# Router of a mixture-of-experts layer: split weights side by side in one stationary tile, ranks in five products

## The reference

```python
logits = xf @ Wr                                   # 4096 x 256 times 256 x 8
probs = jax.nn.softmax(logits, axis=-1)
topk_p, topk_i = jax.lax.top_k(probs, TOP_K)       # 2 of 8
topk_p = topk_p / jnp.sum(topk_p, axis=-1, keepdims=True)
gate = gate.at[jnp.arange(N)[:, None], topk_i].add(topk_p)
for e in range(N_EXPERTS):
    h = new_gelu(xf @ Wfc[e] + bfc[e]) @ Wproj[e] + bproj[e]
    routed = routed + h * gate[:, e:e + 1]
```

## Time and profile before

| what | value |
|---|---|
| median of 3 runs | 934.13 us (933.46 to 935.68) |
| the profiled execution | 939.65 us, its span 938.0 us |
| PE busy in the span | 901.5 us (96%) |
| DVE, ACT, POOL busy | 611.6, 518.8, 338.4 us |
| share of the last chain | PE 86%, DVE 7%, issue 3% |

### The profile page before, as it was taken

The page is one execution under the profiler, slowest core; times in us unless marked ns, Lnnn a source line. Parts: engine busy times, 40 slices in busy tenths (PEclk is TensorE's granted clock), DMA queues, the critical chain, the costliest instruction groups (busy, mean ns, idle before and its releaser), DMA issues.

```text
span 938.0 us, 20267 instructions
## 1 busy us (share of the span) xinstructions
PE 901.5 (96%) x6934; PEld 794.0 (85%) x6943; DVE 611.6 (65%) x1457; ACT 518.8 (55%) x1050; POOL 338.4 (36%) x318
## 2 busy tenths in 40 slices
PE   6999998999998999999999899999999999999996
PEld 4688995566655788888889899999999999999996
DVE  4898796898877766666555655565565656565442
ACT  3693433665546355546444666575666657575552
POOL 3467222211311554544453224233242423332222
PEclk9999999999999999999999899999999999999998
DMA  8300020000002111111237245225252522522222
GB/s 240 123 1 1 1 91 1 2 1 1 2 16 84 49 71 59 65 60 59 77 114 249 58 135 135 47 45 136 46 136 46 136 46 46 136 46 46 46 46 35
DMA packets 48943, 64.00 MB, mean 68 GB/s; under 512 B 9984, under 2 KB 41920, under 8 KB 48768
## 3 DMA queue, kind: packets, MB, share of 16 engines
q0 software_dynamic: 17504, 34.87, 16.0%
q1 hardware_dynamic: 31248, 27.46, 9.9%
q10 hardware_dynamic: 144, 1.05, 0.4%
HBM read 38.59 MB, written 24.77 MB: 68 GB/s over the span
## 4 chain that ended last, share of the span: by engine, by line
PE 86%; DVE 7%; issue 3%; ACT 1%; DMA 1%; POOL 1%; SPq 1%; DVEq 0%; POOLq 0%; ACTq 0%
PE PS L136 24%; PE PS L137 23%; PE PS L138 23%; PE PS L877 3%; PE PS L1833 2%; PE PS L306 2%; PE PS L907 1%; PE PS L921 1%; PE PS L927 1%; DVE mxpad L1121 1%; DVE hidl L142 1%; PE PS L287 1%; DMA xr<-routed_rows 1%; PE PS L1360 1%; PE PS L849 1%
## 5 line engine op out<-in xcount | busy, mean ns | idle before, releaser
L1879 ACT ACTIVATE hideh<-PS,be 128x256 fp32r<-128x256 f32 x280 | 140.5, 502 | 154.2 <-PE PS L138 139.5
L1907 POOL DMA_INDIRECT out_rows<-y,toki x70 | 122.9, 1755 | 270.4 <-DVE y L1947 261.3
L142 DVE TENSOR_TENSOR hidel<-act32e,hideh 128x256 fp32r<-128x256 f32 x280 | 118.4, 425 | 107.5 <-ACT act32e L1881 95.3
L136 PE MATMUL PS<-xTeh,wfch 128*128 128x256 f32 x560 | 159.4, 285 | 1.7 <-issue 1.1
L136 PE MATMUL PS<-wprh,hideh 128*128 128x256 f32 x560 | 159.0, 284 | 0.0
L137 PE MATMUL PS<-xTel,wfch 128*128 128x256 f32 x560 | 158.4, 283 | 0.0
L138 PE MATMUL PS<-xTeh,wfcl 128*128 128x256 f32 x560 | 158.4, 283 | 0.0
L138 PE MATMUL PS<-wprh,hidel 128*128 128x256 f32 x560 | 155.9, 278 | 0.0
L137 PE MATMUL PS<-wprl,hideh 128*128 128x256 f32 x560 | 155.9, 278 | 0.0
L1881 ACT ACTIVATE act32e<-PS,be 128x256 f32<-128x256 f32 x280 | 140.9, 503 | 2.8 <-DVE hidel L142 2.8
L136 PEld LDWEIGHTS PS<-xTeh,wfch 128*128 128x128 f32 x560 | 107.3, 192 | 3.3 <-issue 2.6
(11 more groups left out here) (273 smaller groups left out, 2086.3 us busy)
## 6 DMA issues: line engine op xcount, KB each, us to landing
xr<-routed_rows SPq DMA_DIRECT2D x36, 272.0 KB
fcraw<-in_Wfc POOLq DMA_DIRECT2D x8, 1024.0 KB
prraw<-in_Wproj POOLq DMA_DIRECT2D x8, 1024.0 KB
X<-in_x SPq DMA_DIRECT2D x8, 512.0 KB, 6.6
out_rows<-X SPq DMA_DIRECT2D x8, 512.0 KB, 2.9
routed_rows<-pads SPq DMA_DIRECT2D x8, 272.0 KB
out_rows<-y,toki POOLq DMA_INDIRECT x70
ctx<-in_ctxT SPq DMA_DIRECT2D x4, 256.0 KB, 6.5
```

The lines of the kernel that those rows point to most:

```text
L136: nc.tensor.matmul(out, wh, xh, start=first, stop=False)
L142: return eng.tensor_tensor(out, whole, high.bitcast(F32), ALU.subtract)
L1879: nc.scalar.activation(hid[0][:, j, :], PS[:, j % 4, 0:BLK], ACT.Gelu_apprx_tanh, bias=bias)
L1907: nc.gpsimd.indirect_dma_start(out=out, out_offset=bass.IndirectOffsetOnAxis(ap=toki[:, h:h + 1], axis=0), in_=y[:, h, :], in_offset=None, ...
```

## The change

Two edits. (1) The high and low router weights lie side by side in `both_wr`, 16 columns, and each half of the input is multiplied with all 16: four TensorE products for a batch instead of six (low x low, left out before, is now computed too). `lT` has 16 rows, its transposes 16 columns, and `choose` adds the two halves with a reduction out of PSUM where it copied before. (2) `both` gets a fifth tile that stays zero (a memset in `next_setup`). `ranks` is one product of `both` with the triangle over 40 columns, and then, for each tile s, one product with ones whose moving operand is tile s repeated over all later tiles and the totals (32, 24, 16 and 8 columns). They go to bank 4 instead of 5.

```diff
-            wrp = [early("wr" + n, [P, KD, E], F32R) for n in "hl"]
+            both_wr = early("both_wr", [P, KD, 2 * E], F32R)
...
-            both = early("both", [P, TB, E], BF16)
+            both = early("both", [P, TB + 1, E], BF16)
...
-            lT = late("lT", [E, L])
+            lT = late("lT", [2 * E, L])
...
                 def logits(b):
                     pe.wait_ge(hT_ready, KD * b + KD)
-                    for k in range(KD):
-                        last = product(PS[0:E, 4, :], [w[:, k, :] for w in wrp],
-                                       [x[:, k, :] for x in xTs[b % 2]], k == 0, k == KD - 1)
+                    for i, x in enumerate(xTs[b % 2]):
+                        for k in range(KD):
+                            last = nc.tensor.matmul(PS[0:2 * E, 4, :], both_wr[:, k, :], x[:, k, :],
+                                                    start=i + k == 0, stop=i + k == KD)
...
-                        last = nc.tensor.transpose(PS[:, 5, t * E:(t + 1) * E], lT[0:E, t * P:(t + 1) * P],
-                                                   ident[0:E, 0:E])
+                        last = nc.tensor.transpose(PS[:, 5, 2 * t * E:2 * (t + 1) * E], lT[0:2 * E, t * P:(t + 1) * P],
+                                                   ident[0:2 * E, 0:2 * E])
...
                 def ranks(b):
                     pe.wait_ge(chosen, b + 1)
-                    for t in range(TB):
-                        for s in range(t + 1):
-                            last = nc.tensor.matmul(PS[:, 5, (TB + t) * E:(TB + t + 1) * E],
-                                                    triones[:, 0 if s == t else 1, :], both[:, s, :],
-                                                    start=s == 0, stop=s == t)
+                    end = (TB + 1) * E
+                    nc.tensor.matmul(PS[:, 4, 0:end], triones[:, 0, :], both[:], start=True, stop=False,
+                                     skip_group_check=True)
                     for s in range(TB):
-                        last = nc.tensor.matmul(PS[:, 5, 2 * TB * E:(2 * TB + 1) * E], triones[:, 1, :], both[:, s, :],
-                                                start=s == 0, stop=s == TB - 1)
+                        last = nc.tensor.matmul(PS[:, 4, (s + 1) * E:end], triones[:, 1, :],
+                                                both[:, s:s + 1, :].to_broadcast([P, TB - s, E]),
+                                                start=False, stop=s == TB - 1, skip_group_check=True)
...
                 def choose(b):
-                    nc.vector.tensor_copy(lg[:, 0, :, :].rearrange("p t e -> p (t e)"),
-                                          PS[:, 5, 0:TB * E]).then_inc(l_read, 1)
+                    nc.vector.tensor_reduce(lg[:, 0, :, :],
+                                            PS[:, 5, 0:2 * TB * E].rearrange("p (t c e) -> p t e c", c=2, e=E),
+                                            op=ALU.add, axis=AX).then_inc(l_read, 1)
...
                 def next_setup():
+                    nc.vector.memset(both[:], 0.0)
```

More of the change, by code:

```diff
@@ L1492, in evac_logits @@
                     act.wait_ge(lT_psum, b + 1)
-                    nc.scalar.activation(lT[0:E, :], PS[0:E, 4, :], ACT.Copy).then_inc(lT_ready, 1)
+                    nc.scalar.activation(lT[0:2 * E, :], PS[0:2 * E, 4, :], ACT.Copy).then_inc(lT_ready, 1)
                 def whole(b, first=2):
@@ L1622, in choose @@
                     link(nc.vector.tensor_tensor(m4[:, 2, :], m4[:, 0, :], m4[:, 1, :], ALU.subtract))
-                    nc.vector.tensor_tensor(both[:], oh[:, 0, :, :], oh[:, 1, :, :],
+                    nc.vector.tensor_tensor(both[:, 0:TB, :], oh[:, 0, :, :], oh[:, 1, :, :],
                                             ALU.add).then_inc(chosen, 1)
@@ L1643, in place_rows @@
                     link(nc.vector.tensor_tensor(pos,
-                                                 PS[:, 5, TB * E:2 * TB * E].rearrange("p (t e) -> p t e", e=E),
+                                                 PS[:, 4, 0:TB * E].rearrange("p (t e) -> p t e", e=E),
                                                  carry[:].unsqueeze(1).to_broadcast([P, TB, E]), ALU.add))
-                    nc.vector.tensor_tensor(carry[:], carry[:], PS[:, 5, 2 * TB * E:(2 * TB + 1) * E],
+                    nc.vector.tensor_tensor(carry[:], carry[:], PS[:, 4, TB * E:(TB + 1) * E],
                                             ALU.add).then_inc(r_read, 1)
@@ L1692, in next_split @@
                     dve.wait_ge(wr_in, 16)
-                    nc.vector.tensor_copy(wrp[0][:], wr[:]).then_inc(wr_split, 1)
+                    nc.vector.tensor_copy(both_wr[:, :, 0:E], wr[:]).then_inc(wr_split, 1)
                     dve.wait_ge(wr_split, 1)
-                    low(nc.vector, wrp[1][:], wr[:], wrp[0][:]).then_inc(wr_split, 1)
+                    low(nc.vector, both_wr[:, :, E:2 * E], wr[:], both_wr[:, :, 0:E]).then_inc(wr_split, 1)
                 o_low, att_residual, invert_sums, turn_back, divide = attention[4](dve, next_setup, next_rows, next_split)
```

## The result

The changed kernel takes 932.06 us, median of 20 runs (928.59 to 935.81). The kernel before, in 20 runs beside it, takes 935.50 us (932.79 to 937.38). The ratio is 0.9969, 95% interval 0.9957 to 0.9981: 2.9 us faster (1.8 to 4.0); the two medians lie 3.4 us apart. The forecast was 4.9 us less, 929.2 us, range 926.8 to 931.5, so the time lies 2.9 us above the forecast and 0.6 us above the range.

The account below looks back on a forecast made before the run. TensorE was taken to bound six batches, alternating with VectorE in the first part. Terms 3.7 (logits) + 1.5 (ranks) - 0.1 - 0.1 - 0.1 gave 4.9 us less than 934.13: 929.2 us, range 926.8 to 931.5.

Parts of the forecast that it names:

- 0.463 + 0.21 - 0.02: Savings per batch on TensorE: two fewer logits products 0.463 us, cheaper ranks 0.21, less 0.02 for wider transposes.
- rival C: The five rank products don't pipeline, 166 ns each instead of 30: 934.0 us, no change; chance 0.03.
- rival E: Loads of the rank products are not hidden, nine fewer save 0.86 us a batch: 924.7 us; chance 0.01.
- the unknown terms: Bounds of the uncertain small costs, other than serial ranks: together 0.5 us down and 0.8 up.
- At nothing: Parts counted as costing 0: the 16-row copy, the halves of `both_wr`, bank 4 for the ranks; scattering called untouched.
- this margin: Slack between the gate behind ScalarE's `copy_rows` and VectorE's need of it after `place_slots`; expected to hold, no size given.
- the logits and ranks of batch 1 as on the chain: Batch 1's TensorE savings counted in full: logits in eight batches, 3.7 us; ranks in seven, 1.5 us.
- transposes of batch 2 about 1 us earlier: A sign on TensorE's timeline that the forecast holds, beside the routed stage starting 4.9 us earlier.
- Scattering is not touched: The 16 row copies and DMAs of a batch keep their place behind the slots; counted as no cost.
- rival A: The stall behind the ranks of batch 1 goes, 1.5 us more saved: 927.7 us; chance 0.19.
- rival B: A pause and low clock of that kind elsewhere, costing 1.7 to 3.2 us: 930.9 to 932.4 us; chance 0.10.
- Rival D: Thinner router work lowers TensorE's clock in every batch, 1.7 us a fall: 939.4 us with six; chance 0.03.

Follow-up runs that it names:

- e7_before: The kernel before again, no edit, one run with a second trace: 935.92 us.
- e8_after: The changed kernel again, no edit, one run: 928.94 us.
- e9_after: The changed kernel again, no edit, on another chip: 931.91 us against 938.81 for the kernel before beside it, ratio 0.9927.
- e12_before_filler: The kernel before with 18 unread TensorE products of 256 columns ahead of the transposes of batch 2, as control: ratio 0.9996 to the kernel before.
- e3_again: The changed kernel again, no edit: 932.42 us against 934.95 for the kernel before beside it, ratio 0.9977.
- filler runs: 18 unread TensorE products ahead of the transposes of batch 2: in the changed kernel 930.86 and 932.73 us, in the kernel before ratio 0.9996.
- e4_double: The changed kernel with two buffers for `rows` and `slotc`: 929.48 us, ratio 0.9951 to the kernel before.
- e10_double: The changed kernel with two buffers for `rows` and `slotc`, repeated on another chip: 929.04 us, ratio 0.9908 to the kernel before.
- e14_shift_double: The changed kernel with two buffers plus 24 unread products of 8 columns ahead of the ranks of batch 0: 930.21 us.
- e13_shift: The changed kernel with 24 unread products of 8 columns ahead of the ranks of batch 0: 931.62 us against 932.90 for the changed kernel.
- e15_after: The changed kernel again, no edit: 932.90 us against 935.89 for the kernel before beside it, ratio 0.9976.

## Why the prediction was wrong

**The terms of the sum were right.** A batch was to shrink by 0.463 + 0.21 - 0.02 = 0.65 us and shrank by 0.68; the halves alone read 0.44 and 0.24. The rank products cost 28 ns each on average (0.14 us for five), so they take nothing extra for the repeated operand: rival C's 166 ns is excluded. The Trainium skill's formula for LDWEIGHTS ("TensorE: Matmul & The Clock Gate") gives 107 ns for the load of 128 columns that each has; the trace does not agree that each product takes that long, and rival E, which would have taken 0.86 us off a batch in the ranks' half where 0.24 went, is excluded with it. Two slips in the prediction's sums change nothing in the forecast: with 107 ns and its own seven batches the sum would be near 10 us and not near 11; and the unknown terms add up to about 1.0 us up and not 0.8 (0.3 for the logits, 0.1 for the ranks, 0.3 for the transposes, 0.3 for the first step of the choice).

**The step that failed** is the last sentence of the paragraph "At nothing": "VectorE needs the gate only behind all of `place_slots`, and I expect this margin to hold", and with it the counting of the logits and ranks of batch 1 as on the chain. The prediction named the margin and put no number on it. There was none: the list of waits of the kernel before shows no wait for `hn` in the profiled execution and 0.2 us in e7_before, which means TensorE and the scatter's chain arrived nearly together. From there what TensorE saves in batch 1 turns into a wait: the batch was to shrink by 0.65 us and grew by 0.56 (e7_before to e8_after). The forecast "transposes of batch 2 about 1 us earlier" came out 0.8 later (336.01 against 335.20); each of the two traces has one stretch at 1.2 GHz ahead of that point, from 289 and from 329 us, so the clock does not explain it. Between e7_before and e8_after it was 0.4 us earlier, after the transposes of batch 1 had been 1.0 earlier (311.94 against 312.92).

**"Scattering is not touched"** was the second half of this error. GpSimd's instructions are the same, but the load of TensorE's instructions is a transfer too, and the change moved it onto the scatter. In the traces of the changed kernel the scatter comes 0.7 to 1.3 us later for it, at the only place where TensorE hangs on a scatter: in its first trace the scatter of batch 1 takes even 4.63 us, and TensorE has no wait for it.

**The stretch behind the ranks of batch 1** (rival A) did not settle as one case. A pause of TensorE there was in the traces of e7_before, e9_after, e12_before_filler and others, and in none of the four kernels taken on the chip of e3_again, changed or half changed. Where it is absent, the wait for `hn` is longer (2.7 us against 1.5 in e9_after with 1.8 us of pauses): one stands for the other, since both end at the scatter's chain. From the transposes of batch 1 to those of batch 2 it takes 21.76 us in e3_again, without a pause, and 21.79 in e8_after, with 0.8 us of short pauses. This argues that A would have given nothing without the second buffer; no run removed the pause alone.

**The clock** (rival B) took another part. The profiled changed kernel has stretches at 0.50 (1.2 GHz) from 289, 337 and 518 us in the shared stage, where that of before has them from 329 and 520. Over all runs with a recorded clock in sets of six or more the mean is 0.9918 in the changed kernel (50 runs) and 0.9927 in the kernel before (92 runs), which is worth 0.9 us; 20 of the 50 have no clock of the kernel before beside them. It is 0.0018 and 0.0015 lower on two chips, and 0.0014 higher on the chip of e9. Its cause is open: the filler runs do not bear out the one that was tried, e4_double has the low clock too (0.9917) though its wait is gone, e10_double and e14_shift_double on other chips have not (0.9940, 0.9932), and neither half alone has it. Rival D did not occur; the clock of the six batches is 0.99 with one such stretch.

**Together**: 4.9 forecast, less 0.65 for the saving of batch 1 that ends in the wait, less 0.56 by which that batch grew, for the most part by the late scatter (3.18 instead of 2.45 us), is 3.7 us; by time x clock the three sets read 3.6 to 4.8. Less 0.9 for the clock it is 2.8, where the ratio gave 2.9 and the medians 3.4. These parts are of the size of the intervals, so this sum is an account, not a proof of each part; the wait is shown by the kernels with two buffers, the late scatter by the rows of e13_shift.

The range failed for two reasons: no rival had the saving end in a wait at batch 1, and it was set from a median of three runs of the kernel before, 1.4 us below that of twenty, with only about 1 us for the spread of the runs. From the median of twenty the same sum would have forecast 930.6 us, and the measured time would have lain inside the shifted range.

## What to carry to other kernels

When a saving is counted batch by batch, look at each batch's waits alone: an engine that already comes to a wait together with what it waits for saves nothing by coming earlier, and "margin" needs a number. Removing instructions also moved the fetches of the instruction stream here, and a fetch beside a scatter went with a scatter 0.7 to 1.3 us longer; where a wait hangs on one small DMA, look for the instruction packet beside it. A repair that is worthless in the old kernel (the second buffer: 0 us) can be worth 2.7 to 2.9 us in the new one, so it is tried again after each gain.

## What the runs showed of the hardware

- A load of TensorE's instructions delays scatters. The 13 traces of kernels with one buffer (before, changed and varied) hold 91 releases of ScalarE by a batch's last scatter. Where a q8 packet starts between the issue of that scatter and 2.4 us after it (16 cases), the release comes 2.99 to 4.64 us after the issue in 15 cases and 2.60 in one; in the other 75, two with a packet that starts 0.2 us ahead of the issue among them, it is at most 2.60 and nearly always 2.44 to 2.48. The packet itself takes 0.9 to 1.5 us of one of the 16 DMA engines (1.4% of 16 x 3.8 us, 14.8% and 19.1% of 16 x 0.5 us in the views above). The count of 91 is a correlation over all places; e13_shift moved one packet on purpose. The Trainium skill says in "DMA: Bandwidth & Descriptors", under why a DMA increments its semaphore by 16, that every one of the engines must report before the data count as landed. The trailing packets of the map after, behind which the release came, fit that; no view here shows which engine they ran on.
- The runs of one kernel spread by their clock. e15_after reads 928.79 us at a mean clock of 0.996 and 936.31 at 0.989: (0.996 - 0.989) x 932 = 6.5 of the 7.5 us.
- The same kernel before took 934.95, 935.78, 935.89 and 938.81 us (medians of 17 to 29 runs) on four chips, the changed one 931.91 to 932.90 on three of them. Part of the difference is the clock: by time x clock the four are 928.4, 928.8, 928.7 and 929.8 us. A gain of 0.3% is not one number for all chips.
- The cause of the pause behind the ranks of batch 1 stays open: in e7_before VectorE reads the ranks at 328.96 us, just after GpSimd's power instruction (327.80, 1.05 us) is over, in e8_after at 328.18 (327.08, 1.05 us), with TensorE at rest in part of that time; in e3_again the same instruction runs at 326.34 us without a pause.
